# Five drains of the Pool queue placed among the result scatters of a routed-expert kernel

## The reference

```python
h = tdnn(x)                      # 5 frames side by side @ W + b, relu, batch norm
h = h + attn(layernorm(h))       # 8 heads of 16, a bias for each key column out of an edge list
h = h + ffn(layernorm(h))        # top-1 of 8 experts:
#   logits = xf @ Wr + br; gate = softmax over the one chosen logit (so 1)
#   out[row] = relu(xf @ W1[e] + b1[e]) @ W2[e] + b2[e],  e = argmax(logits[row])
```

## Time and profile before

| | us |
|---|---|
| median of three executions | 265.02 |
| the profiled execution | 264.41 |
| its span, first to last instruction | 262.7 |

### The profile page before, as it was taken

The page is one execution under the profiler, slowest core; times in us unless marked ns, Lnnn a source line. Parts: engine busy times, 40 slices in busy tenths (PEclk is TensorE's granted clock), DMA queues, the critical chain, the costliest instruction groups (busy, mean ns, idle before and its releaser), DMA issues.

```text
span 262.7 us, 8986 instructions
## 1 busy us (share of the span) xinstructions
PE 235.0 (89%) x2852; PEld 199.1 (76%) x2852; DVE 180.2 (69%) x679; ACT 166.4 (63%) x405; POOL 145.0 (55%) x275
## 2 busy tenths in 40 slices
PE   2999798999999999999999896975988999999970
PEld 2946475787888878888787684675987999999960
DVE  3898446577887978879778887674574656565640
ACT  2964355577787776876767556755265777777720
POOL 8101732255557787777877633657647645454550
PEclk9999999999999999999999999998599999999996
DMA  4020199400000111101011014432214644341000
GB/s 122 4 82 0 21 357 296 138 2 0 5 15 27 30 32 42 42 20 40 22 41 42 19 41 103 127 78 58 79 51 129 175 129 113 91 114 57 26 3 0
DMA packets 14461, 18.20 MB, mean 69 GB/s; under 512 B 3991, under 2 KB 10555, under 8 KB 14416
## 3 DMA queue, kind: packets, MB, share of 16 engines
q1 hardware_dynamic: 10976, 11.23, 15.4%
q0 software_dynamic: 3296, 6.00, 7.8%
q10 hardware_dynamic: 144, 0.41, 0.5%
HBM read 10.58 MB, written 7.54 MB: 69 GB/s over the span
## 4 chain that ended last, share of the span: by engine, by line
PE 72%; DVE 9%; issue 5%; ACT 5%; POOL 2%; DMA 1%; DVEq 1%; ACTq 1%; POOLq 1%
PE psS L1242 11%; PE psB L1143 10%; PE psS L1159 7%; PE psO L1284 6%; PE psS L1169 5%; PE psB L1232 4%; PE psU L1232 4%; PE psO L1232 4%; ACT patT L493 3%; PE psU L1274 3%; PE psO L1262 2%; DVE nmax L942 2%; PE psB L1149 2%; PE psB L1127 2%; PE psU L1268 2%
## 5 line engine op out<-in xcount | busy, mean ns | idle before, releaser
L438 POOL DMA_INDIRECT out<-y_out,sidx x38 | 37.1, 977 | 30.5 <-DVE y_out L871 23.9
L942 DVE TENSOR_REDUCE nmax<-psS 121x8 f32<-121x968 f32 x32 | 37.2, 1164 | 15.2 <-PE psS L1169 13.8
L605 ACT ACTIVATE PT<-psS 121x968 f32<-121x968 f32 x32 | 31.3, 977 | 17.2 <-DVE nmax L942 14.8
L431 POOL DMA_INDIRECT region_d<-rows,pos x32 | 34.5, 1078 | 12.2 <-issue 10.9
L1242 PE MATMUL psS<-xgT,W_tile 128*128 128x128 f32 x304 | 41.2, 279 | 0.0
L881 DVE TENSOR_SCALAR hT<-psS,b1T 128x128 f32<-128x128 f32 x76 | 23.3, 347 | 24.8 <-PE psS L1242 23.6
L1242 PEld LDWEIGHTS psS<-xgT,W_tile 128*128 128x128 f32 x304 | 38.1, 197 | 0.0
L568 ACT ACTIVATE hT<-psS,b1T 128x128 f32<-128x128 f32 x76 | 23.8, 364 | 16.1 <-PE psS L1242 15.8
L553 ACT ACTIVATE W_tile<-W_sb 128x512 f32 x38 | 23.9, 630 | 6.6 <-issue 4.5
L1159 PE MATMUL psS<-kT,qT 32*121 32x121 f32 x512 | 22.3, 288 | 1.3 <-ACT PT L605 0.7
L1159 PEld LDWEIGHTS psS<-kT,qT 32*121 32x121 f32 x512 | 16.5, 179 | 8.7 <-issue 6.2
(11 more groups left out here) (257 smaller groups left out, 560.8 us busy)
## 6 DMA issues: line engine op xcount, KB each, us to landing
xg<-region_d SPq DMA_DIRECT2D x38, 129.0 KB, 2.3
W_sb<-in_L_ffn_W SPq DMA_DIRECT2D x1, 2048.0 KB, 9.2
region_d<-pads SPq DMA_DIRECT2D x1, 1032.0 KB, 7.3
out<-y_out,sidx POOLq DMA_INDIRECT x38, 2.4
b_bc<-in_L_ffn_b SPq DMA_DIRECT2D x1, 512.0 KB, 5.2
region_d<-rows,pos POOLq DMA_INDIRECT x32
xs<-in_x ACTq DMA_DIRECT2D x1, 402.5 KB, 3.8
edge_i<-in_L_attn_edge_index SPq DMA_DIRECT2D x1, 64.0 KB, 4.0
```

The lines of the kernel that those rows point to most:

```text
L431: pool.indirect_dma_start(region_d, bass.IndirectOffsetOnAxis(pos[0:L, b:b + 1], 0), rows[0:L, b, E:E + ROW], None, bounds_check=E * CAP - ...
L438: pool.indirect_dma_start(out, bass.IndirectOffsetOnAxis(sidx[:, s:s + 1], 0), y_out[:, u, :], None, bounds_check=N - 1, oob_is_err=False) ...
L605: act.activation(PT[0:L, b % 2, :, :, :], score_half(1), ACT.Exp).then_inc(s_exp, 1)
L942: dve.tensor_reduce(nmax[0:L, :].rearrange("p (j c) -> p j c", c=HB)[:, :, HD + 1:HD + 3], score_half(0), AX.X, ALU.max, negate=True).then ...
```

## The change

One `drain` instruction of Pool is put behind result `s` where `s % 6 == 5` and `s + 3 < NT`. With 38 tiles that is behind results 5, 11, 17, 23 and 29. It signals nothing and no other engine waits for it. Nothing else is changed.

```diff
@@ -477,6 +477,8 @@
                 if s < ALONG:
                     pool.wait_ge(f_y, s + 4)
                 scatter_out(s)
+                if s % 6 == 5 and s + 3 < NT:
+                    pool.drain()
```

## The result

The changed kernel took 262.25 us as the median of 15 executions, against 265.69 us for 15 of the kernel before. The ratio is 0.9875 with a 95% interval of 0.9842 to 0.9908: 3.3 us less, 2.4 to 4.2. It is taken without the executions that fell into a slower state of the chip, so it isn't quite the quotient of the two medians. The forecast was 4.2 us less; the 262.25 us lie inside its range of 260.0 to 262.4, near the upper end. In the profiled executions the span fell from 262.7 to 258.7 us.

What follows compares the result with a forecast made beforehand. TensorE was taken to hold 72% of the span, with Pool's end drain as pure tail. Middle drains cost 0 and the end gains 4.2 us: 260.8 us from 265.02, range 259.8 to 270.5, the likeliest reading's own 260.0 to 262.4.

Steps and rivals of the forecast that it cites:

- The tail as the place of the gain: Pool's drain at the block's end: 4.74 us after the last landing is pure tail; span ends 4.2 us earlier, at 258.5.
- Proportional to the DMAs since the drain before: Likeliest reading of Pool's drains: work counts DMAs since the previous drain, 0.067 us each; 260.0 to 262.4 us, chance 0.50.
- the fixed price: Rival: every Pool drain after any DMA costs the same, up to 5.87 us; 272 to 279 us, chance 0.20.
- half and half: Rival: half of the end drain's 4.74 us is fixed, a middle drain takes 4.0 us; 262.4 to 267.5, chance 0.08.
- the whole program's count: Rival: a drain's price follows all DMAs issued so far, 3.2 up to 5.2 us; about 270 us, chance 0.06.
- a price of the block's end: Rival: the long part belongs to the block's end, not the drain; nothing happens, 264.7 to 265.4 us, chance 0.16.
- The rule of the Trainium skill: Rule against the forecast: preamble and postamble drains take about 12 ns; five add 0.06 us, time stays 265.0.
- The size of a DMA's share: Pool's drain work per DMA: 4.74 / 71 = 0.067 us, plus 1.4 us waiting for the scatter just issued.
- The price in the middle: Five added drains on Pool: first 4.0 us, the other four 1.8 each, together 11.2 us, all hidden.
- The cover: Slack hiding the middle drains: loads keep 5.5 and 9.4 us in hand, Pool on time by result 32, last scatter stays.
- The sum: Whole program: middle costs 0, end drain's work falls from 4.74 to 0.53 us; span 4.2 us earlier, 260.8 us.

## Why the prediction was right, and where its steps were off

**The tail as the place of the gain: right.** The last result landed at 258.2 and the drain ended at 258.5, where before they stood at 257.7 and 262.4. The span came out at 258.7 against 258.5. Of the 1.45 us between the forecast median and the measured one, 0.7 lie in the kernel before, 265.02 us then and 265.69 over 15 executions.

**Proportional to the DMAs since the drain before: right, and shown.** Doubled drains (47 ns), drains with one and with six DMAs (0.07 and 0.28 us behind the landing), one drain behind the last result (7132 and then 47 ns) and twelve extra DMAs (82 ns each) leave no room for the fixed price, for half and half, for the whole program's count or for a price of the block's end. The rule of the Trainium skill that was weighed in the prediction, about 12 ns for such drains ("VectorE: DVE Perf Modes", section "The DRAIN you can't avoid"), comes nearest to a Pool drain without DMAs since the drain before, 47 ns, and doesn't hold for one with 71, 7132 ns.

**The size of a DMA's share: the term that was mis-sized.** The prediction took 4.74 / 71 = 0.067 us, counted from the landing, with the whole landing wait in front of it. Measured are 0.083 us counted from the end of the last scatter's issue (71, 63, 39, 32 and 83 DMAs: 5.87, 5.22, 3.26, 2.67 and 6.86 us). Where the last transfer landed late, the drain ended at the landing plus about half of that: 1.89 us for 45 DMAs (half of 3.73 is 1.87), 1.65 for 39 (1.62), 0.78 for 18 (0.75), 0.36 for 8 (0.33), 0.28 for 6 (0.25). So the later of the two holds: 83 ns for each DMA from the end of issue, or the landing plus 41 ns for each and 0.03 us besides. That one half needs the landing and the other doesn't is worked out from these numbers; what Pool does in either is not shown by any run. For the end it made the work 0.36 us where 0.53 was forecast, and the first drain 3.3 us where 4.0 was.

**The price in the middle: too low for three of the four later drains.** Forecast 1.8 us each, measured 3.04, 3.49, 1.58 and 2.14. Their work, 0.28 us, is below the forecast 0.4; the wait is above it: results 11 and 17 landed 3.7 and 4.2 us after their issue, where the prediction took the median of 2.4 and knew a highest of 3.4. Those rows hold only the landings that were recorded. In before, load 25 waits for result 13, issued at 210.83; SP's wait for it ended at 214.58, 3.75 us later, so a longer landing could have been read there. And the first scatter behind each of the five drains starts 0.87 us after the drain's end (203.05 to 203.92, 246.26 to 247.13), where the prediction put the 0.30 us between two scatters in a row. The prediction had said that a second drain as long as the first would prove it wrong; it was (3.04 and 3.26), by a late landing and not by a fixed price. That test was badly chosen, since it didn't part the landing from the work.

**The cover: nearly right.** TensorE never waited, tiles 11 to 37 take 48.5 us as before. But Pool wasn't on time again by result 32: result 30 started 4.1 us later than in the earlier trace rows, where 1.2 was forecast, and the last scatter came 1.46 us behind the last `y_out` in place of 0.92, 0.5 us of the gain. Going through Pool's queue with before's starts (an estimate), the measured drains with 0.57 us more behind each make result 30 4.0 us late and the last 0.4. Without the 0.57, or with it and the forecast drains, the last is on time: it took both, the late landings and the later starts. In the two kernels with two drains, where Pool is on time when the last drain comes, this part is 0.

**The sum.** Span: 4.2 forecast, 3.9 measured: 0.5 lost to the late last scatter, 0.2 won back by the shorter end work, the last `y_out` 0.1 earlier. By the medians 3.4.

## What to carry to other kernels

Look at what ends last before looking at what is busiest: Pool was on 2% of the chain, and its drain at the end of the block held the end up for 4.7 us behind the last landing, because the DMAs issued from Pool leave work that a drain does by the piece. Draining earlier, where Pool has slack, moves that work off the end, and here two drains left a shorter tail than five (3.6 us against 4.1; the times can't tell them apart) and than one (4.8 and 5.25 us). Each drain also waits for its last transfer, and one that has many DMAs to work off near the end, or stands too close behind another, makes the last result late. Price a drain as the later of two things, the work behind the issue and the landing plus a part of the work, and take the landing from its worst rows, not from its median.

## What the runs showed of the hardware that wasn't expected

Where its last transfer lands early enough, a Pool drain costs 83 ns for each DMA issued from Pool since the drain before, counted from the end of issue, for DMAs of one element as for those of 128 rows, in a straight proportion from 32 to 83 DMAs. Where it lands late, the drain ends at the landing plus about half of that, from 0.07 us for one DMA to 1.89 for 45. Right behind another drain it costs 47 ns. A drain's record begins while earlier scatters are still being issued, so its recorded length (7.55 us behind result 11) can be more than twice the time from the end of issue to its end (3.04 us). After a drain the next scatter starts 0.87 us later, 0.57 more than after another scatter.
